# Ternary feed-forward layer: the two 16-bit parts of a tile's gelu rows turned by one transfer in place of two

## What is computed

```python
def absmax_quant(x):
    gamma = jnp.max(jnp.abs(x), axis=-1, keepdims=True)
    x_hat = jnp.clip(x * Q_B / gamma, -Q_B + EPS, Q_B - EPS)
    return x_hat * gamma / Q_B

def bitlinear(x, w):
    xn = layer_norm(x)
    x_hat = xn + jax.lax.stop_gradient(absmax_quant(xn) - xn)
    w_hat = w + jax.lax.stop_gradient(ternarize_weights(w) - w)
    return jnp.einsum('bsd,od->bso', x_hat, w_hat)

h = bitlinear(x, w_fc)                 # 512 -> 2048
h = jax.nn.gelu(h, approximate=False)
return bitlinear(h, w_proj)            # 2048 -> 512
```

## Time and profile before

| | |
|---|---|
| median of 3 runs | 1742.95 us (1738.2 to 1748.8) |
| the profiled execution | 1737.88 us, of which the span from first to last instruction is 1736.1 us |
| mean granted TensorE clock | 0.973 of full speed |
| PE busy | 1582.6 us (91%) |
| DVE, ACT, POOL busy | 1177.1, 933.7, 574.8 us |
| the ternary layer | from 671.2 us (first product) to 907.4 us (last product) of the span |
| products of the layer | 512 at L1068 and 512 at L1078, 128x512 each |
| transposing transfers at L1046 | 32 |

### The profile page before, as it was taken

The page is one execution under the profiler, slowest core; times in us unless marked ns, Lnnn a source line. Parts: engine busy times, 40 slices in busy tenths (PEclk is TensorE's granted clock), DMA queues, the critical chain, the costliest instruction groups (busy, mean ns, idle before and its releaser), DMA issues. The chain is left out here.

```text
span 1736.1 us, 33561 instructions
## 1 busy us (share of the span) xinstructions
PE 1582.6 (91%) x12554; PEld 802.2 (46%) x12554; DVE 1177.1 (68%) x2076; ACT 933.7 (54%) x1641; POOL 574.8 (33%) x581
## 2 busy tenths in 40 slices
PE   5899999899999987999979999687898899999997
PEld 3533333364333333444434444454565566666564
DVE  4599998458999964999866777796623243333387
ACT  5756777345677844777735665477232333333332
POOL 4556575171000021232222111496182111111265
PEclk9999999999999998999999999798999999999999
DMA  7422332000000011665548999562071765456344
GB/s 240 138 46 57 74 69 49 2 2 2 2 2 2 2 14 43 125 120 120 92 85 280 356 338 359 189 196 73 23 133 44 277 234 169 151 185 219 103 123 134
DMA packets 177841, 211.42 MB, mean 122 GB/s; under 512 B 114202, under 2 KB 117624, under 8 KB 175504
## 3 DMA queue, kind: packets, MB, share of 16 engines
q1 hardware_dynamic: 170336, 188.54, 36.3%
q0 software_dynamic: 7344, 20.73, 4.5%
HBM read 193.33 MB, written 56.40 MB: 144 GB/s over the span
## 5 line engine op out<-in xcount | busy, mean ns | idle before, releaser
L704 ACT ACTIVATE layer_scratch<-layer_banks 128x512 f32<-128x512 f32 x576 | 312.5, 595 | 136.4 <-PE layer_banks L601 134.9
L810 DVE TENSOR_REDUCE layer_mx<-layer_banks 128x2 f32<-128x1024 f32 (+3 forms) x304 | 339.2, 1155 | 24.1 <-PE layer_banks L579 20.6
L2202 PE MATMUL sparse_ps_g<-wgate,sparse_xT 128*128 128x352 f16 x1128 | 184.2, 313 | 1.6 <-DVE sparse_xT L2280 1.6
L616 PE MATMUL layer_banks<-layer_scratch,V 128*32 128x256 f32 x2304 | 174.6, 389 | 0.8 <-ACT layer_scratch L712 0.8
L1321 PE MATMUL lin_ps_z<-arena,early 128*128 128x512 f16 x576 | 134.9, 385 | 7.6 <-DVE lin_relu L1469 4.1
L2202 PEld LDWEIGHTS sparse_ps_g<-wgate,sparse_xT 128*128 128x128 f16 x1128 | 108.4, 98 | 62.0 <-DVE sparse_xT L2280 2.0
L2286 DVE SCALAR_TENSOR_TENSOR sparse_hid<-sparse_th,sparse_ps_g 128x352 f32<-128x352 f32 x47 | 24.5, 521 | 150.9 <-ACT sparse_th L2247 150.9
L2313 POOL DMA_INDIRECT xg<-x_d,token x45 | 42.5, 945 | 248.2 <-PE sparse_ps_x L2192 248.2
L1078 PE MATMUL ffn_ps_y<-wprojT,ffn_hT 128*128 128x512 f16 x512 | 115.6, 385 | 8.0 <-DMA ffn_hT<-ffn_h 8.0
L1068 PE MATMUL ffn_ps_fc<-wfcT,early 128*128 128x512 f16 x512 | 114.4, 382 | 5.8 <-PEq L934 3.4
L579 PE MATMUL layer_banks<-KT,arena 64*128 64x512 f16 (+3 forms) x768 | 113.8, 330 | 5.9 <-DVE layer_mx L810 5.8
(11 more groups left out here) (305 smaller groups left out, 3124.6 us busy)
## 6 DMA issues: line engine op xcount, KB each, us to landing
wgate<-gate_d SPq DMA_DIRECT2D x47, 1408.0 KB
wdown<-down_d SPq DMA_DIRECT2D x47, 768.0 KB
lin_sp_raw<-in_L_ffn_w_gate_up_dram SPq DMA_DIRECT2D x56, 352.0 KB, 5.3
gate_d<-lin_sp_parts SPq DMA_DIRECT2D x56, 352.0 KB, 5.0
y_d<-y SPq DMA_DIRECT2D x47, 256.0 KB, 4.9
down_d<-lin_sp_parts SPq DMA_DIRECT2D x42, 256.0 KB, 5.0
lin_sp_raw<-in_L_ffn_w_down_dram SPq DMA_DIRECT2D x28, 256.0 KB, 5.3
wfcT<-in_L_ffn_w_fc_dram SPq DMA_DIRECT2D x8, 512.0 KB, 7.1
```

Source lines behind the costliest of these rows:

```text
L616: last = pe.matmul(ps_o[32 * jj:32 * jj + 32, 256 * half:256 * half + 256], V[:, kt, 4 * jg + jj, :], prob[(2 * q + jj // 2) % 4][:, half, ...
L704: act.activation(prob[g % 4][:, par, :, :], ps_t[:, (2 * g + par) % 3, :, :], ACT.Exp, scale=HD ** -0.5).then_inc(exp_done, 1)
L810: dve.tensor_reduce(mx[x % 2][:, c, :, at:at + per], ps_s[:, 2 * (r % 2):2 * (r % 2) + 2, 0:per * n].rearrange("p e (h k) -> p e h k", k=n ...
L2202: last = pe.matmul(ps_g[u][n][rows, :], xT[u][:, a, k, rows], w, start=(k == 0 and i == 0), stop=(k == KC - 1 and i == 2), skip_group_chec ...
```

## The change

The two transfers `ht(0)` and `ht(1)` become one `ht`, which turns the whole of `h2[u]` (128 x 4096 columns) into the whole of `hT[u]`. It is issued once `hl_done` has counted hlo(t), so after both parts are written. There is one semaphore for each parity in place of two, and all who waited for one of the two wait for it: `proj(t)` once, ahead of its first product, and `hhi` and `hlo` before they write into `h2` again.

```diff
-        ht_in = [[f.sem(f"ht_in{u}{part}") for part in range(2)] for u in range(2)]
+        ht_in = [f.sem(f"ht_in{u}") for u in range(2)]
...
-                def ht(part):
-                    def fn(t):
-                        u = t % 2
-                        sp.wait_ge(hl_done if part else hh_done, t + 1)
-                        after(sp, y_done, t - 1)
-                        sp.dma_start_transpose(out=hT[u][:, part, :, :], in_=h2[u][:, part, :]).then_inc(ht_in[u][part], 16)
-                    return fn
+                def ht(t):
+                    u = t % 2
+                    sp.wait_ge(hl_done, t + 1)
+                    after(sp, y_done, t - 1)
+                    sp.dma_start_transpose(out=hT[u][:, :, :, :].rearrange("p a k c -> p (a k) c"),
+                                           in_=h2[u][:, :, :].rearrange("p a n -> p (a n)")).then_inc(ht_in[u], 16)
...
-                unrolled(NT + AHEAD, [(0, of_layer(next_layer)), (3, xt), (5, of_layer(ht(0))), (5, of_layer(ht(1)))])
+                unrolled(NT + AHEAD, [(0, of_layer(next_layer)), (3, xt), (5, of_layer(ht))])
...
                     after(pe, r_done, t - 1)
+                    pe.wait_ge(ht_in[u], 16 * (t // 2 + 1))
                     for part in range(2):
-                        pe.wait_ge(ht_in[u][part], 16 * (t // 2 + 1))
                         for k in range(NK):
...
-                    after(act, ht_in[u][0], 16 * (t // 2))
+                    after(act, ht_in[u], 16 * (t // 2))
...
-                    after(dve, ht_in[u][1], 16 * (t // 2))
+                    after(dve, ht_in[u], 16 * (t // 2))
```

## The result

The changed kernel takes 1753.49 us (median of 8 runs, 1751.8 to 1762.8), against 1743.82 us for the kernel before (8 runs). The ratio is 1.0062, with a 95% interval of 1.0043 to 1.0080: about 11 us slower (7.5 to 14), where +9.5 us was forecast. The profiled execution has a span of 1751.2 us, 15.1 more than before, and that is not all the change's doing. The layer, from its first product to the end of its last, took 236.1 us (671.20 to 907.32) and now takes 247.0 (671.49 to 918.53): +10.9. The layer starts 0.3 us later, and what follows it took 3.9 us more. Counted from the first product of the next phase to the end of the span, that last part ranges from 825.3 us (the kernel before) to 836.3 us (e11) in the profiled executions of this document, with no edit in it.

The account below looks back on a forecast made before the run. The prediction took PE to bound the layer's middle and the chain from gelu to proj its ends. Front 7.2 and back 2.3 us gave +9.5: 1737.9 became 1747.4, and 5.1 more for the median 1752.4, range 1746 to 1760.

Parts of the forecast that it names:

- The bound: Whole layer: PE bounds the middle, the chain from gelu through the turn to proj bounds the two ends.
- The length of the merged turn: Transfer of 4096 columns: lands 6.9 us after its issue, between bounds of 4.4 and 8.8.
- Rival C: Merged turn: the wider transfer moves faster, so the change is not slower by 0.5%; chance 0.10.
- D: Start at half clock: it is short, costing 1.4 us in place of 2.4; +8.5 us, 1751.4, chance 0.08.
- E: Merged turn: lands late, after 8.8 us, so the middle is overrun too; +16.9 us, 1759.8, chance 0.09.
- Front: Ahead of proj(0): start 4.75 us later, plus 2.4 for starting at half clock; 7.2 us.
- Middle: Tiles between the ends: PE doesn't wait, as 8.2 us are left for a turn of 6.9; 0.
- SP's queue: SP's issues: one less for each tile, the next loads issued up to 2 us later, but hidden; 0.
- Back: proj(14) and proj(15): proj(15) starts 4.75 us later but wins 2.4 by staying at full clock; +2.3 us.
- rival B: Ahead of proj(15): the short gap cools the clock, so the 2.4 isn't won; +11.9 us, 1754.9, chance 0.22.
- the sum: Whole kernel: front 7.2 and back 2.3 us add to +9.5 us, 1752.4; chance 0.45.
- The next phase: After proj(15): starts 3.46 us after it, at half clock as before; 0.

Follow-up runs that it names:

- e11: Kernel before, with only tiles 8 to 13 turned by one transfer each; layer 238.9 us against 236.1, one run of 1754.1 us.
- e2: Kernel before, with tiles 0 to 13 turned by one transfer each, 14 and 15 by two; layer 242.5 us against 236.1, ratio 1.0041.
- e3: Kernel before, with only tiles 14 and 15 turned by one transfer each; layer 241.6 us against 236.1, ratio 1.0021.
- e12: Kernel before, with only tile 13 turned by one transfer; layer 236.1 us, as before, one run of 1737.8 us.
- e4: Kernel before, with tiles 1 to 13 turned by one transfer each, 0, 14 and 15 by two; layer 239.3 us against 236.1, ratio 1.0020.
- e1: Kernel before, still two transfers, but the first held back until the low part is written too; layer 240.2 us against 236.1, ratio 1.0031.
- e7: Kernel before, with parts at tiles 0, 14 and 15 written and turned in halves of 1024 columns; layer 233.5 us against 236.1, ratio 0.9984.
- e5: Changed kernel, with spare products filling PE's gaps ahead of proj(0), proj(14) and proj(15); layer 243.1 us against 247.0, ratio 1.0033 to the kernel before.

## Why the prediction was right

*The bound* (PE in the middle, landings at the ends) held: e2 and e3 place the whole loss at the ends, e12 shows a merged turn that costs nothing.

*The length of the merged turn:* 6.9 was taken, 6.7 measured, at the rate of the two turns before (211 and 215 GB/s). One of 16 took 8.5 (tile 1), more than the 7.8 allowed for. It was still in time: it was issued at 709.56, so it landed at 718.1, and proj(1) came at 719.89. Rival C is out. Rivals D and E are out too: the start at half clock cost 2.3 us at proj(0) and 2.5 at proj(14), not 1.4, and the turns took 6.7 us, not 8.8. The 350 GB/s and more that the Trainium skill gives for such transposes (DMA: Bandwidth & Descriptors, Latency and other measured facts) is not seen in any run here.

*Front:* +4.75 + 2.4 = 7.2. The prediction gives 2.4 us for the stretch from PE's stop at 696.09 to 698.70; it is 2.6, and no term hangs on it. Between fc(2) and proj(0) the starts are 14.40 us apart in place of 9.78, +4.6, and proj(0) is 2.27 longer: 6.9.

*Middle:* 0, with 1.3 us to spare. Measured 0; at tile 8 the turn issued at 808.16 lands at about 814.9 (with the median 6.7) and proj(8) starts at 816.58, 1.7 to spare. e4 and e11 add what the prediction didn't say in numbers: how much the middle costs when the front hasn't paid.

*SP's queue:* the merged issue takes 4.8 us and not the 1.9 to 3.8 of the forecast, a mis-sized term that stays hidden, since no wait for xT appears in the middle.

*Back:* +2.3 was forecast, from +4.75 for the later start and -2.4 for the clock of proj(15). The later start measured +4.7 (proj(15) starts 238.3 us after the layer's first product in place of 226.6, 6.9 of it from the front and 0.1 from before fc(2)). The clock term was mis-sized: proj(15) took 8.75, so -0.75. That is nearer to rival B than to the sum, and with 0.1 + 6.9 + 4.7 - 0.75 it makes the layer 10.9 longer in place of 9.5. What a short gap does to the clock is not settled by its length: over these runs the clock fell around gaps of 2.30 (changed kernel), 2.60 and 2.71 (e3) and 2.87 us (e1), and stayed full after 2.70, after 2.68, 2.70 and 2.72 ahead of proj(0) in e4, e11 and e12, after 3.11 (e4, proj(1)) and 3.29 (e1, proj(15)). What decides it is open.

*The next phase:* 0. It started at full clock this time (36 products in 7.93 us, 10.71 before), and still its last product at L1320 came 178.0 us after its first, 177.2 before: nothing was won. The other 3.1 us by which the part after the layer was longer lie further on, and no experiment was made on them; the spread of that part over these kernels, none of which edits it, is larger than that.

*The number:* 1752.4 was forecast and 1753.49 measured. Part of that closeness is luck: the clock term of proj(15) was too good by 1.7 us, and the medians of the two kernels lie 9.7 us apart where the layers in their traces differ by 10.9.

## What to carry to other kernels

Two transfers that follow each other on the same data path can be as fast as one: here the two turns had landed 6.7 us after the first was issued (694.36 to 701.1), and the merged one takes 6.7 too. The first of the two lets its reader start; merging them delays the reader by the time in which the second part is produced plus the time in which it moves (2.3 + 2.3 us here). Read the price at the ends of a pipelined loop, where nothing else covers it, and ask of the middle how far the late engine lies behind the others: a late transfer is paid once, when that distance is built up, and not again in each tile. For the same reason a gain at the first tile is lost again if another chain of engines sets the pace of the last.

## What the runs showed of the hardware

The gap ahead of proj(0), 2.70 us in the kernel before and 2.71 in e3, left the clock full in one run and at half in the other (proj(0) 7.08 and 8.77 us), though e3 edits nothing there. A start of proj from half clock cost 1.4 us (e3, proj(15)) to 2.5 us (changed kernel, proj(14)) here. There is one trace of each kernel; that executions of one kernel differ by such starts at the three gaps of the layer is likely from this, but not shown.

A turn occupied SP's queue for 1.2 to 1.3 us with 1024 columns (e7), for 1.9 in the median with 2048 (1.3 to 3.0), and for 4.7 to 5.4 with 4096: in the median one issue of 4096 (4.8) takes longer than two of 2048 (3.8). In the three windows over such a transfer the data started about 1.2 us after the issue, and moved at 191 GB/s (xT), 211 and 215. In each of the changed kernel, e2, e4, e5 and e11 the slowest merged turn took 7.4 to 8.5 us to land, where the median is 6.7 or 6.8.
